# Keys of fifteen items as three passes over high and low parts, w1 in two refilled buffers, and another order of the slot

## The reference

```python
for i in range(6):
    xn = _layernorm(x, ln1_w[i], ln1_b[i])
    q, k, v = heads(xn @ wq[i]), heads(xn @ wk[i]), heads(xn @ wv[i])
    q = softmax(q, axis=-1); k = softmax(k, axis=-2)
    context = einsum('bhnd,bhne->bhde', k, v)
    attn = einsum('bhnd,bhde->bhne', q, context)
    x = merge(attn) @ wo[i] + bo[i] + x
    xn = _layernorm(x, ln2_w[i], ln2_b[i])
    hdn = xn @ w1[i]                        # 128 -> 512
    hdn = where(hdn >= 0, hdn, 0.01 * hdn)
    x = hdn @ w2[i] + x
```

## Time and profile before

| | us |
|---|---|
| median of 3 runs (lowest, highest) | 593.21 (592.42, 593.96) |
| the profiled execution | 592.57 |
| its span, first to last instruction | 590.8 |
| busy: TensorE | 576.9 (98%) |
| busy: VectorE | 487.5 (83%) |
| busy: ScalarE | 434.0 (73%) |
| busy: GpSimd | 328.8 (56%) |

### The profile page before, as it was taken

The page is one execution under the profiler, slowest core; times in us unless marked ns, Lnnn a source line. Parts: engine busy times, 40 slices in busy tenths (PEclk is TensorE's granted clock), DMA queues, the critical chain, the costliest instruction groups (busy, mean ns, idle before and its releaser), DMA issues.

```text
span 590.8 us, 12241 instructions
## 1 busy us (share of the span) xinstructions
PE 576.9 (98%) x4166; PEld 514.2 (87%) x4166; DVE 487.5 (83%) x828; ACT 434.0 (73%) x763; POOL 328.8 (56%) x396
## 2 busy tenths in 40 slices
PE   8999999999999999999999999999999999999997
PEld 7899887988978989889889889898898898798886
DVE  4887898989878888889879889788898797787675
ACT  3678595876876877877868768768778687687762
POOL 6996146747854864342442552443524767877762
PEclk9999999999999999999999999999999999999999
DMA  8309242323423344545355445445442442432202
GB/s 273 85 35 305 72 152 90 134 85 122 136 81 117 120 113 143 151 117 162 108 143 164 124 127 150 108 153 167 101 161 69 115 149 80 126 130 70 71 37 107
DMA packets 74944, 73.18 MB, mean 124 GB/s; under 512 B 27265, under 2 KB 65153, under 8 KB 74882
## 3 DMA queue, kind: packets, MB, share of 16 engines
q1 hardware_dynamic: 72400, 68.18, 37.6%
q0 software_dynamic: 2048, 4.20, 2.4%
q10 hardware_dynamic: 434, 0.02, 0.0%
HBM read 39.87 MB, written 32.51 MB: 122 GB/s over the span
## 4 chain that ended last, share of the span: by engine, by line
PE 71%; DMA 11%; ACT 5%; issue 4%; DVE 4%; POOL 3%; SPq 2%; ACTq 0%; DVEq 0%; POOLq 0%
PE psY L525 20%; PE psT L538 7%; PE psS L570 5%; PE psM L550 5%; PE psH L418 5%; PE psH L419 5%; PE psH L420 5%; PE psT L413 5%; DMA through<-blocks 5%; PE psT L604 4%; DMA turned<-through 4%; DMA through<-turn 2%; SPq L321 2%; ACT xnT L994 2%; PE psM L474 2%
## 5 line engine op out<-in xcount | busy, mean ns | idle before, releaser
L525 PE MATMUL psY<-w_all,hid 128*128 128x128 f32 x1536 | 187.3, 275 | 0.9 <-DVE hid L1532 0.9
L525 PEld LDWEIGHTS psY<-w_all,hid 128*128 128x128 f32 x1536 | 180.9, 192 | 4.4 <-issue 1.4
L1532 DVE TENSOR_TENSOR hid<-psH,hsl 128x512 f32<-128x512 f32 x192 | 127.6, 678 | 23.5 <-ACT hsl L948 23.0
L948 ACT ACTIVATE hsl<-psH 128x512 f32<-128x512 f32 x192 | 108.0, 591 | 36.8 <-PE psH L420 33.8
L2105 POOL TENSOR_TENSOR qsm<-qe,qrec 128x1024 f32<-128x1024 f32 x24 | 46.6, 1940 | 110.2 <-DVE qrec L1608 110.1
L2083 POOL TENSOR_TENSOR xn_lo<-xn,xn_hi 128x512 fp32r<-128x512 f32 x48 | 60.9, 1286 | 67.3 <-ACT xn_hi L1012 67.3
L418 PE MATMUL psH<-xn_hi,w_hi 128*128 128x512 f32 x192 | 86.1, 449 | 0.7 <-DVE hid L1532 0.7
L978 ACT ACTIVATE xh<-X,shift,rstd 128x128 f32<-128x128 f32 x188 | 77.0, 483 | 5.0 <-POOL shift L2012 5.0
L419 PE MATMUL psH<-xn_hi,w_lo 128*128 128x512 f32 x192 | 76.0, 396 | 0.0
L420 PE MATMUL psH<-xn_lo,w_hi 128*128 128x512 f32 x192 | 75.7, 394 | 0.0
L2008 POOL TENSOR_TENSOR rstd<-veps,minus_half 128x8 f32<-128x8 f32 x44 | 73.5, 1670 | 0.0
(11 more groups left out here) (150 smaller groups left out, 980.5 us busy)
## 6 DMA issues: line engine op xcount, KB each, us to landing
through<-turn SPq DMA_DIRECT2D x22, 512.0 KB, 2.7
turn<-through SPq DMA_DIRECT2D x88, 128.0 KB
through<-blocks SPq DMA_DIRECT2D x20, 512.0 KB
turned<-through SPq DMA_DIRECT2D x80, 128.0 KB, 3.0
wb<-expert_rows SPq DMA_DIRECT2D x40, 128.0 KB, 2.1
sorted_x<-blocks SPq DMA_DIRECT2D x5, 512.0 KB, 5.5
xs_xsT<-sorted_x SPq DMA_DIRECT2D x40, 64.0 KB, 2.5
sorted_y<-ys SPq DMA_DIRECT2D x10, 256.0 KB, 2.4
```

Of the source, the lines that this page charges most:

```text
L525: last = nc.tensor.matmul(tile(psY, t), tile(hid[:, c, :], t), w2_all[:, n // NBATCH, c, :], start=(c == 0 and t == 0), stop=(c == NC - 1) ...
L948: nc.scalar.activation(hsl[:, i % 2, :], psH[:, i % 2, :], ACT.Copy, scale=SLOPE) \
L1532: nc.vector.tensor_tensor(hid[:, i % NC, :], psH[:, i % 2, :], hsl[:, i % 2, :], ALU.max) \
```

## The change

Keys of items 9 to 23 are taken by split_product, from xnT_hi and xnT_lo (high_input on ScalarE, low_input on GpSimd) and wk_hi and wk_lo (stage_wk on VectorE, split_wk on GpSimd, once per layer, two buffers). w1 is no longer held whole: w1_f has two buffers, and load_layer on SP refills one. In the slot the calls stand in another order on every engine. The core of the diff:

```diff
+            def load_layer(l):
+
+                sp.wait_ge(sig("w1_staged"), l - 1)
+                sp.dma_start(w1_f[:, l % 2, :], w1[l]).then_inc(sig("layer_loaded"), 16)
@@ slot of SP @@
             def slot(s):
-                groups(s)
                 feature_major2(s - 2)
                 feature_major1(s)
+                groups(s)
+                if s % NBATCH == 1 and (s + 3) // NBATCH < L:
+                    load_layer((s + 3) // NBATCH)
@@ keys of TensorE @@
                     for h in (0, 1):
-                        last = nc.tensor.matmul(psT[:, h * HALF:(h + 1) * HALF], wk_all[:, n // NBATCH, :],
-                                                xnT[:, h * HALF:(h + 1) * HALF], start=True, stop=True)
+                        cols = slice(h * HALF, (h + 1) * HALF)
+                        if split_keys(n):
+                            pe.wait_ge(sig("xnT_lo_ready"), 2 * split_before(n) + h + 1)
+                            last = split_product(psT[:, cols], wk_hi[:, l % 2, :], wk_lo[:, l % 2, :],
+                                                 xnT_hi[:, cols], xnT_lo[:, cols])
+                        else:
+                            last = nc.tensor.matmul(psT[:, cols], wk_all[:, l, :], xnT[:, cols], start=True, stop=True)
@@ slot of TensorE @@
                 output(s - 4, 7)
-                if group_of(s) is not None:
-                    apply_expert(group_of(s))
                 hidden(s - 3, 0)
                 hidden(s - 3, 1)
-                keys(s - 1)
                 queries(s - 1)
                 hidden(s - 3, 2)
                 hidden(s - 3, 3)
+                output(s - 3, 0)
+                keys(s - 1)
+                output(s - 3, 1)
+                output(s - 3, 2)
+                hidden(s - 3, 4)
+                if group_of(s) is not None:
+                    apply_expert(group_of(s))
                 keys_by_token(s - 1)
-                output(s - 3, 0)
-                output(s - 3, 1)
+                hidden(s - 3, 5)
+                output(s - 3, 3)
                 key_sums(s - 1)
-                output(s - 3, 2)
+                queries_by_feature(s - 1)
                 context(s - 1)
-                hidden(s - 3, 4)
-                hidden(s - 3, 5)
+                hidden(s - 3, 6)
                 mixing(s - 1)
-                output(s - 3, 3)
-                queries_by_feature(s - 1)
-                hidden(s - 3, 6)
                 hidden(s - 3, 7)
...
+            def high_input(n):
+
+                if split_keys(n):
+                    act.wait_ge(sig("xnT_ready"), n + 1)
+                    for half in range(2):
+                        cols = slice(half * HALF, (half + 1) * HALF)
+                        nc.scalar.activation(xnT_hi[:, cols], xnT[:, cols], ACT.Copy).then_inc(sig("xnT_hi_ready"), 1)
@@ slot of ScalarE @@
                 hidden_input(s - 3)
-                if s > 4:
-                    attention_input(s - 1)
+                attention_input(s - 1)
+                high_input(s - 1)
                 slope(s - 3, 0)
                 slope(s - 3, 1)
                 norm2(s - 2, 0)
                 norm2(s - 2, 1)
-                if s != ITEMS + 1:
-                    norm2(s - 2, 2)
-                exp_keys(s - 1)
-                if s != ITEMS + 1:
-                    norm2(s - 2, 3)
+                norm2(s - 2, 2)
                 slope(s - 3, 2)
+                norm2(s - 2, 3)
+                exp_queries(s - 1)
                 slope(s - 3, 3)
-                keys_by_token(s - 1)
-                exp_queries(s - 1)
                 norm1(s, 0)
                 norm1(s, 1)
+                exp_keys(s - 1)
                 norm1(s, 2)
                 norm1(s, 3)
+                keys_by_token(s - 1)
                 slope(s - 3, 4)
...
+            def low_input(n, half):
+
+                if split_keys(n):
+                    pool.wait_ge(sig("xnT_hi_ready"), 2 * split_before(n) + half + 1)
+                    cols = slice(half * HALF, (half + 1) * HALF)
+                    nc.gpsimd.tensor_tensor(xnT_lo[:, cols], xnT[:, cols], xnT_hi[:, cols].bitcast(F32), ALU.subtract) \
+                        .then_inc(sig("xnT_lo_ready"), 1)
```

More of the change, by code:

```diff
@@ L1259, in _ @@
             attention_input(23)
+            high_input(23)
             slope(21, 0)
@@ L2202, in _ @@
             move_rows(9, 1)
+            split_wk(2)
             scale_queries(8)
@@ L2226, in _ @@
             low_part(21, 1)
+            low_input(23, 0)
+            low_input(23, 1)
             deviations2(22)
```

85 lines of the change are left out of this document (59 added, 26 removed).

## The result

| | before | after |
|---|---|---|
| median of 4 runs each (lowest, highest), us | 593.37 (592.42, 593.96) | 616.08 (615.80, 617.85) |
| ratio, 95% interval | | 1.0388 [1.0365, 1.0412] |
| profiled execution (span) | 592.57 (590.8) | 615.81 (613.8) |

What follows compares the result with a forecast made beforehand. TensorE was taken as the bound, busy 230.35 of 231.46 us in ten slots. Stalls of 3.8 (slots 11 to 20), 7.6 (21 to 23), 2.2 and 1.0 (ends) sum to 14.6 us: 607.5 us, range 595 to 616.

Steps and rivals of the forecast that it cites:

- what the change takes off TensorE: Keys: six passes, 1.41 us instead of 1.72, 4.7 us over 15 items; 3.3 us of waits for xnT can go too.
- Ten expert slots: Slots 11 to 20: key_sums stalls 0.7 us for ys behind VectorE's row; slots of 23.45 us, +3.8 us with casts.
- The casts of wk: VectorE, three of the ten expert slots: 0.25 us each ahead of the bias.
- Slots 21 to 23: Late store and GpSimd's gathers delay low_part and deviations1; +4.3, +2.1 and +1.2 us, +7.6 together.
- rival C: Every slot behind xnT, hidden 2 close behind hidden 1: 0.5 us more in 14 slots, 614; covers falling clock; chance 0.15.
- The rule cited from the Trainium skill: TensorE too idle for some microseconds falls to 1.2 GHz; in slots 21 to 23 a few us per slot.
- Ends: Slot 24: deviations2(22) late on GpSimd, +2.2 us; slot 10: +1 us, bounds -0.8 and 1.5.
- the refills: w1 refills, three more 256 KB DMAs on SP: costed at 0; uncovered, each an issue of 0.34 us.
- A (the saving stays): All three engines keep up: 582.6 us; decided by whether the bias lands before q0+11.35; chance 0.12.
- B (597.4, gathers absorbed): Only the bias wait stalls the ten slots, TensorE's later start absorbs the gathers: 597.4 us; chance 0.18.

Runs made afterwards that it cites:

- combined2: combined plus the third gather pair behind scale_queries and, in slot 24, exp_keys(23) between the second and third part of norm2(22): 594.88 us, ratio 1.0032.
- combined2_unsplit: combined2 without the split of the keys (f32 keys for all items, no calls for wk): 595.90 us, ratio 1.0050.
- bias_early: Changed kernel with VectorE's expert_bias one place earlier, ahead of blocks_of_norm1 and the cast of wk: 610.32 us, ratio 1.0302.
- order_alone: Changed kernel without the split of the keys; new slot order and two w1 buffers stay: 602.36 us, ratio 1.0159.
- no_gathers: Changed kernel with all 32 gather DMAs of the expert rows left out: 603.90 us, ratio 1.0179.
- gathers_behind: Changed kernel with only the second pair of gathers moved behind deviations1 and low_part(s-3,1): 606.83 us, ratio 1.0244.
- store_early: Changed kernel with the last store of sorted_y issued ahead of the four quadrants of feature_major1(20): 612.57 us, ratio 1.0327.
- the second trace: Changed kernel run once more without an edit: 611.42 us in its one run.
- w1_alone: Kernel before with w1 in two refilled buffers and nothing else changed: 592.97 us, ratio 1.0018.
- combined4: combined3 with keys(23) behind hidden blocks 2 and 3, last gathers ahead of weigh(2), wk's cast and subtraction later in the prologue: 598.00 us, ratio 1.0095.
- old_order: The split and two w1 buffers in the slot order of the kernel before: 676.78 us, ratio 1.1398.
- combined: Changed kernel with bias and last store earlier, second gathers behind low_part, split_wk behind scale_queries, slot 24's slopes ahead of norm2: 596.12 us, ratio 1.0053.
- combined3: combined2 with deviations2(22) ahead of gathers, weigh(0) and low_input on GpSimd, and ScalarE's slot 24 order of the changed kernel: 595.14 us, ratio 1.0042.

## Why the prediction fell short

**What bounds the kernel, and what the change takes off TensorE: right in kind, the passes worth less.** Keys went from 1.72 us to six passes in 1.47 (forecast 1.41), and the waits for xnT went. With the stalls out (combined2) ten slots are 3.5 us shorter. Of these, 1.9 us come from the passes, where 3.1 were forecast, and 1.7 from the order (combined2_unsplit).

**Ten expert slots: right in mechanism, 1.4 us short.** TensorE waits ten times for ys, 0.6 to 0.7 us. bias_early removes the wait, order_alone shows that VectorE's row sets the slot. The casts of wk were laid at 0.25 us in three slots and cost 0.12 to 0.15 (order_alone). The slot came out at 23.67 instead of 23.45: the passes save 0.25 us instead of 0.31, and a wait costs some 0.2 us beyond its own length (0.8 us gained for 0.6 of waiting in bias_early), where 0.1 was laid.

**Slots 21 to 23: the step that failed.** Forecast +7.6, measured +13.1. The mechanism was named rightly (late store, gathers ahead of low_part and deviations1, waits for xn_lo and expk): no_gathers removes the whole term, gathers_behind and store_early their parts. What failed is that the sum laid the clock at nothing. The prediction left its fall to rival C, with 0.15 for the whole rival, since the granted clock in the earlier trace rows is 1.00 throughout, and put it at "a few us per slot". It fell once in each slot, 3.41 us at half speed. By the pairs of slots above the falls cost 2.1 us in slot 22, 1.2 in slot 23 and next to nothing in slot 21, 3.3 of the 5.5 us that are missing. Without a fall, slots 22 and 23 took 24.8 and 25.0 us in other traces, against 24.9 to 25.0 forecast.

The other 2.2 us are not the clock's. A further 1.4 us of slot 22 (28.33 against 26.91 in bias_early, with the same calls and a fall) belong to that execution, as the second trace shows; why TensorE's releases came late there stays open. Slot 21 is 0.9 us over: its key transposes start 20.3 us into the slot (forecast 20.0), and the rest of it takes 7.7 us instead of 7.1.

The rule cited from the Trainium skill (TensorE: Matmul & The Clock Gate, Part 1), that a TensorE too idle falls back to 1.2 GHz, agrees with the falls to 0.50 in this trace. That the clock had stayed up in the earlier trace rows was no evidence against it: the longest wait in the earlier trace rows is 1.2 us, and in 37 of 80 other executions of the kernel before the mean clock was below 0.999.

**Ends: nearly right in size.** Slot 24 +2.0 for +2.2 (the prediction's own terms, 2.7 less 0.3, make 2.4), slot 10 +1.2 for +1. In the second trace slot 10 took 22.61 us, as before the change, so the +1.2 is not firm. Missing was the 1.4 us ahead of slot 10. w1_alone excludes the refills (slot 10 starts at 207.15 us). Much of the scatter of that start over the variants is the clock's: it is 206.9 to 209.0 us in the ten traces of changed kernels without a fall before slot 10, 209.0 to 210.3 in the five with one at 22 to 40 us, and 212.4 with two. The changed kernel's own 208.41 and 207.75 have none. What puts them 0.7 to 1.4 us behind the 207.03 of before is not shown; combined4, with the casts and subtractions of wk later, has 206.86.

**The rivals.** A (the saving stays) needed the bias early, as the prediction said, and the gathers elsewhere too; even combined2, which has both, did not reach the kernel before. B (597.4, gathers absorbed) needed a GpSimd that hides them in every slot; order_alone's slots 22 and 23 come near that, the changed kernel's don't. C (614, "also covers a clock that falls") came nearest in time, by its clock and not by its stated mechanism: hidden 2 waiting for hid is not there (0.2 us in all). The forecast's terms for slots 11 to 20 and for the ends came within 1.5 us each, so the miss is mostly that of slots 21 to 23.

## What to carry to other kernels

Where TensorE is busy for 99% of a loop, an order that leaves it idle for 2 us at one place costs the wait and, about every second time here, another 1.2 to 2.1 us in clock, unless a later wait swallows them. Look for such places in the slots where one engine has extra instructions, here the gathers. An instruction that a slower engine issues for later use (a gather, a cast) belongs behind those that TensorE waits for in the same slot, and the edit should move it alone: 1.28 us in front of deviations1 cost more than the repair gained. A stall can hide the next one (split_wk under ys), so the price of a repair is read from the new trace, not from the sum of waits. And one trace is one execution: the mean granted clock of the untraced runs tells whether it was a typical one.

## What was not expected of the hardware

- The granted clock fell to 0.50 for 3.41 us (three times for 6.83 in old_order), and not behind every long wait. Leaving old_order out, the traces have 30 waits of TensorE of 1.77 to 2.7 us from 200 us on; a fall began within the wait or up to 2.1 us behind it in 16 of them. Waits of 2.03 us in slot 23 brought one in store_early and none in bias_early, and in old_order waits of 3.15, 3.14 and 3.18 us (slots 14, 15 and 22) passed without one. No fall between slot 10 and the end of slot 24 was without such a wait or a longer one; the shortest was 1.77 us (slot 24 of combined).
- The same changed kernel took 611.4 us once and 615.8 to 617.9 four times. Which waits bring a fall explains only part of it: the execution of 611.4 us and one of 616.35 have the same mean clock, 0.994.
- VectorE's product of two SBUF tiles (gate, X: 128x1024) took 1.22 us before the change. Where it began beside a GpSimd weigh it grew with the time that they shared: 1.30 us for 0.2 us beside it (the changed kernel), 1.60 for 0.5 (combined4), 1.83 for 0.75 (combined2) and 2.66 for 1.6 (combined3), nearly as if it stood still meanwhile. Where a gather's issue began second, it was the one that stretched, to 1.79 to 2.03 us instead of 0.95 to 1.08. VectorE's operations that read PSUM kept their lengths beside GpSimd's (hid 0.65 to 0.71 us), and so did its reduces and 32x32 transposes of one SBUF tile (1.17 to 1.25 us). The small cast of wk, from SBUF to SBUF, took 0.22 us away from GpSimd's weighings and subtractions and 0.41 beside them (combined3).
- An f32 product of 128 columns is two records and 0.22 us; a float32r pass of 512 columns is one record and 0.235 us.
